# Gated cross-attention and expert block on one Trainium2 core: the attention update's bias, scale, statistics and normalisation moved between engines

## The reference

```python
hs = layernorm(x)
q, k, v = hs @ Wq.T + bq, ctx @ Wk.T + bk, ctx @ Wv.T + bv       # 16 heads of 32
probs = softmax(clip(where(mask, q @ k.T / sqrt(32), -1e4), -50, 50))
delta = clip(residual_scale, 0, 0.3) * ((probs @ v) @ Wo.T + bo)
delta = (delta - mean(delta)) / sqrt(var(delta) + 1e-5) * ln_gamma + ln_beta
x1 = x + tanh(g_xattn) * delta
h = layernorm(x1)                                                 # "h" in the kernel
out = x1 + tanh(g_ffn) * top2_of_8_experts(h)                     # router, silu(gate) * up, down
```

## Time and profile before

| | us |
|---|---|
| median of 3 runs | 996.5 (996.27 to 996.64) |
| the profiled execution | 1003.46 |
| its span, first to last instruction | 1001.7 |
| PE busy in the span | 918.4 |
| DVE busy | 471.9 |
| ACT busy | 369.5 |
| POOL busy | 256.3 |

### The profile page before, as it was taken

How to read it: one execution, slowest core, us unless ns; L and a number is a source line. 1 busy time by engine, 2 the same in 40 slices (tenths; PEclk the granted TensorE clock), 3 DMA queues, 4 the chain that set the end, 5 groups by cost and what they waited for, 6 DMA issues and landing times.

```text
span 1001.7 us, 14294 instructions
## 1 busy us (share of the span) xinstructions
PE 918.4 (92%) x4201; PEld 717.9 (72%) x4202; DVE 471.9 (47%) x796; ACT 369.5 (37%) x701; POOL 256.3 (26%) x285
## 2 busy tenths in 40 slices
PE   4979999996744999999999999999999999999994
PEld 3746667664523888888888888888888888888883
DVE  5547978777778312253263172531361254217211
ACT  3555454532132222262262262622352253226221
POOL 4033627264204121131121221312122122122121
PEclk9989998989766999999999999999999999999998
DMA  7030130203364412145153162541272136111121
GB/s 299 4 123 0 54 116 31 95 22 105 139 201 147 147 32 32 21 157 158 26 194 116 34 217 85 179 135 32 40 264 41 22 105 210 21 33 30 21 42 21
DMA packets 27904, 93.92 MB, mean 94 GB/s; under 512 B 5424, under 2 KB 5424, under 8 KB 21104
## 3 DMA queue, kind: packets, MB, share of 16 engines
q1 hardware_dynamic: 18528, 72.03, 19.4%
q0 software_dynamic: 8640, 20.62, 11.1%
q10 hardware_dynamic: 720, 1.07, 0.3%
HBM read 75.03 MB, written 18.68 MB: 94 GB/s over the span
## 4 chain that ended last, share of the span: by engine, by line
PE 80%; issue 6%; DVE 6%; POOL 2%; DMA 2%; ACT 2%; SPq 0%; DVEq 0%; POOLq 0%; ACTq 0%
PE bank L247 71%; PE bank L1284 3%; DMA xs<-in_x 2%; PE bank L1271 2%; PE bank L1157 1%; DVE rden L390 1%; DVE xr L410 1%; PE bank L1111 1%; PE bank L1123 1%; PE bank L1144 1%; DVE st L425 1%; POOL rs L747 1%; ACT hs L881 1%; PE bank L1075 1%; POOL o_lo L739 0%
## 5 line engine op out<-in xcount | busy, mean ns | idle before, releaser
L247 PE MATMUL bank<-g_hi,gt_hi 128*128 128x512 f32 x592 | 237.5, 401 | 1.6 <-DVE gt_lo L658 1.6
L247 PE MATMUL bank<-g_hi,gt_lo 128*128 128x512 f32 x592 | 234.3, 396 | 0.0
L247 PE MATMUL bank<-g_lo,gt_hi 128*128 128x512 f32 x592 | 234.3, 396 | 0.0
L688 DVE TENSOR_TENSOR hid<-silu,bank 128x256 f32<-128x256 f32 x148 | 61.4, 419 | 308.8 <-ACT silu L1037 308.8
L1037 ACT ACTIVATE silu<-bank 128x256 f32<-128x256 f32 x148 | 56.7, 383 | 255.9 <-PE bank L247 255.9
L247 PEld LDWEIGHTS bank<-g_hi,gt_hi 128*128 128x128 f32 x592 | 111.4, 188 | 27.5 <-issue 2.0
L247 PEld LDWEIGHTS bank<-g_hi,gt_lo 128*128 128x128 f32 x592 | 111.4, 188 | 27.2
L247 PEld LDWEIGHTS bank<-g_lo,gt_hi 128*128 128x128 f32 x592 | 111.6, 189 | 25.8
L843 POOL COPY g_idx<-slot_idx 128x1 int32 x37 | 6.9, 185 | 470.9 <-ACT w_nxt L1051 470.9
L247 PE MATMUL bank<-dn_hi,hd_hi 128*128 128x512 f32 x296 | 126.4, 427 | 0.0
L247 PE MATMUL bank<-dn_lo,hd_hi 128*128 128x512 f32 x296 | 116.6, 394 | 0.0
(11 more groups left out here) (218 smaller groups left out, 1308.2 us busy)
## 6 DMA issues: line engine op xcount, KB each, us to landing
raw<-in_w_exp SPq DMA_DIRECT2D x48, 1024.0 KB, 5.3
raw<-in_w_attn SPq DMA_DIRECT2D x4, 1024.0 KB, 13.6
xs<-in_x SPq DMA_DIRECT2D x4, 1024.0 KB, 6.5
xr<-in_x SPq DMA_DIRECT2D x4, 1024.0 KB, 6.2
out_rows<-xr SPq DMA_DIRECT2D x16, 256.0 KB, 2.0
h_rows<-dh SPq DMA_DIRECT2D x16, 256.0 KB, 2.1
rows<-in_b_rows ACTq DMA_DIRECT2D x1, 1024.0 KB, 13.5
c_raw<-in_ctx_t SPq DMA_DIRECT2D x1, 640.0 KB, 4.0
```

The lines of the kernel that those rows point to most:

```text
L247: mm = eng.matmul(psum, a(k), b(k), start=(first and k == 0 and j == 0), stop=(last and k == n - 1 and j == 2))
L688: dve.tensor_tensor(hid[:, p, :], silu[:, p, :], bank[p][:, 256:512], ALU.mult).then_inc(hid_done, 1)
```

## The change

1. bo enters as one more matmul of each `o_product`: the stationary tile `two_rows` is one in rows 0 and 32 and zero elsewhere, `bo_two` holds the high half of the scaled bo in row 0, its low half in row 32, and zero elsewhere.
2. The residual scale is multiplied into Wo when its halves are made.
3. The bank then holds the scaled update itself. bn_stats reads it from the bank, and (update - mean) * gamma reads it from there too; L417 and `d_ready` are gone. The bank is free after the latter (`dgam`).
4. h is normalised by ACT as x * rsh + (-mean * rsh); POOL makes the second factor, `nmh`. `normalised` is gone from DVE.
5. In the tail, ACT's order is changed: the four `normalise_h` come in, and `first_gu(1)` goes behind the last copy of h.
6. c_raw shares its memory with later tiles.

```diff
         def split_weight(w):                                    # DVE
             dve.wait_ge(w_hi_done, w + 1)
-            dve.tensor_tensor(lo, raw[:, w, :], f32(hi), ALU.subtract).then_inc(w_lo_done, 1)
+            if w == 3:
+                dve.scalar_tensor_tensor(out=lo, in0=raw[:, w, :], scalar=tg[:, 2:3], in1=f32(hi),
+                                         op0=ALU.mult, op1=ALU.subtract).then_inc(w_lo_done, 1)
+            else:
+                dve.tensor_tensor(lo, raw[:, w, :], f32(hi), ALU.subtract).then_inc(w_lo_done, 1)
...
             if u is not None:                                   # DVE, update_and_residual
-                dve.wait_ge(h_store, (n + 1) * 16 * TT)
                 dve.wait_ge(d_mm, n * TT + u + 1)
-                dve.scalar_tensor_tensor(out=dh[:, u, :], in0=bank[2 + u % 2][:, :], scalar=tg[:, 2:3],
-                                         in1=rows[:, 1, :], op0=ALU.mult, op1=ALU.add).then_inc(d_ready, 1)
+                dve.bn_stats(st6[:, u, :], bank[2 + u % 2][:, :]).then_inc(dstats, 1)
...
-            if u is not None:
-                dve.wait_ge(d_ready, n * TT + u + 1)
-                dve.bn_stats(st6[:, u, :], dh[:, u, :]).then_inc(dstats, 1)
...
-                dve.scalar_tensor_tensor(out=dh[:, u, :], in0=dh[:, u, :], scalar=mv[:, u, 0:1],
+                dve.wait_ge(h_store, (n + 1) * 16 * TT)
+                dve.scalar_tensor_tensor(out=dh[:, u, :], in0=bank[2 + u % 2][:, :], scalar=mv[:, u, 0:1],
                                          in1=rows[:, 2, :], op0=ALU.subtract, op1=ALU.mult).then_inc(dgam, 1)
-        def normalised(n, t):
-            dve.wait_ge(hrstd, n * TT + t + 1)
-            dve.tensor_scalar(dh[:, t, :], xr[:, t, :], mvh[:, t, 0:1], rsh[:, t:t + 1],
-                              ALU.subtract, ALU.mult).then_inc(h_done, 1)
...
+        dve.wait_ge(setup, 16)                                  # DVE, set-up, ahead of k_all
+        dve.tensor_scalar(bo_two[0:1, :], rows[0:1, 1, :], 1.0, None, ALU.mult).then_inc(bo_done, 1)
+        dve.tensor_scalar(bo_two[LO_ROW:LO_ROW + 1, :], rows[LO_ROW:LO_ROW + 1, 1, :], 1.0, None,
+                          ALU.mult).then_inc(bo_done, 1)
+        dve.wait_ge(bo_done, 2)
+        dve.tensor_tensor(bo_two[LO_ROW:LO_ROW + 1, :], rows[LO_ROW:LO_ROW + 1, 1, :],
+                          f32(bo_two[LO_ROW:LO_ROW + 1, :]), ALU.subtract).then_inc(bo_done, 1)
...
-        for tile in (kbd_hi, kbd_lo, vbd_hi, vbd_lo, hsel):     # POOL
+        for tile in (kbd_hi, kbd_lo, vbd_hi, vbd_lo, hsel, two_rows, bo_two):
             pool.memset(f32(tile[:]), 0.0).then_inc(setup, 1)
...
+        for i, row in enumerate((0, LO_ROW)):
+            pool.wait_ge(setup, 14 + i)
+            pool.memset(f32(two_rows[row:row + 1, :]), 1.0).then_inc(setup, 1)
...
             pool.tensor_tensor(rsh[:, t:t + 1], veh[:, t:t + 1], mhalf[:, 0:1], ALU.pow).then_inc(hrstd, 1)
+            plain(pool)
+            pool.wait_ge(hrstd, n * TT + t + 1)
+            pool.tensor_scalar(nmh[:, t:t + 1], mvh[:, t, 0:1], rsh[:, t:t + 1], -1.0,
+                               ALU.mult, ALU.mult).then_inc(hbias, 1)
...
             hi = weight_halves[w][0].rearrange("p k n -> p (k n)")   # ACT, split_weight
-            act.activation(hi, raw[:, w, :], ACT.Copy).then_inc(w_hi_done, 1)
+            if w == 3:
+                act.wait_ge(dset, 1)
+                act.activation(hi, raw[:, w, :], ACT.Copy, scale=tg[:, 2:3]).then_inc(w_hi_done, 1)
+            else:
+                act.activation(hi, raw[:, w, :], ACT.Copy).then_inc(w_hi_done, 1)
+        def normalise_h(n, t):
+            act.wait_ge(x1_done, n * TT + t + 1)
+            act.wait_ge(hbias, n * TT + t + 1)
+            act.activation(dh[:, t, :], xr[:, t, :], ACT.Identity, scale=rsh[:, t:t + 1],
+                           bias=nmh[:, t:t + 1]).then_inc(h_done, 1)
...
+                if 4 <= s < 8 and back:                         # ACT, batch: behind exp and ex_hi
+                    normalise_h(b - 1, s - 4)
                 if s == 3 and front:
                     normalise_x(b + 1)
                 if s == 4 and front:
...
         act.wait_ge(d_mm, NT)                                   # ACT, tail
+        normalise_h(NB - 1, 0)
         first_gu(0)
+        normalise_h(NB - 1, 1)
         h_copy(NB - 1, 0, tail=True)
-        first_gu(1)
+        normalise_h(NB - 1, 2)
         h_copy(NB - 1, 1, tail=True)
+        normalise_h(NB - 1, 3)
         h_copy(NB - 1, 2, tail=True)
         h_copy(NB - 1, 3, tail=True)
+        first_gu(1)
         first_gu(2)
...
             if t >= 2:                                          # PE, o_product
-                pe.wait_ge(d_ready, n * TT + t - 1)
+                pe.wait_ge(dgam, n * TT + t - 1)
...
-                              n=1, first=(k == 0), last=(k == KC - 1))
-            mm.then_inc(d_mm, 1)
+                              n=1, first=(k == 0), last=False)
+            pe.matmul(bank[2 + t % 2][:, :], two_rows[:, :], bo_two[:, :], start=False, stop=True).then_inc(d_mm, 1)
```

More of the change, by code:

```diff
@@ L39 @@
 HW = H + E
+LO_ROW = 32
 def flamingo_gated_block(nc, x, ctx_t, mask, w_attn, b_cols, b_rows, gates, gate_t, w_exp, out):
@@ L109, in flamingo_gated_block @@
         k_all = sb("k_all", [P, KC, NB * T], F32, pa)
+        crs = ExitStack()
+        c_raw = sb("c_raw", [P, KC, CT], F32, crs)
+        crs.close()
         v_all = sb("v_all", [P, NB + 1, H], F32, pa)
@@ L116, in flamingo_gated_block @@
         hsel = sb("hsel", [P, P + NH], F32R, pa)
+        two_rows = sb("two_rows", [P, P], F32R, pa)
+        bo_two = sb("bo_two", [P, H], F32R, pa)
         bsel = sb("bsel", [NH, KC, 4, HD], F32R, pa)
@@ L142, in flamingo_gated_block @@
         rsh = sb("rsh", [P, TT], F32, pa)
+        nmh = sb("nmh", [P, TT], F32, pa)
         mhalf = sb("mhalf", [P, TT], F32, pa)
@@ L222, in flamingo_gated_block @@
              "inverse_spread", "context_normalised", "o_hi_done", "o_lo_done"))
-        d_mm, d_ready, dstats, dmean, dvar, drstd, dgam, xb_done, x1_done = (sem(n) for n in
-            ("delta_product", "delta_scaled", "delta_stats", "delta_mean", "delta_var", "delta_rstd",
+        d_mm, dstats, dmean, dvar, drstd, dgam, xb_done, x1_done = (sem(n) for n in
+            ("delta_product", "delta_stats", "delta_mean", "delta_var", "delta_rstd",
              "delta_gamma", "x_with_beta", "x1_done"))
-        hstats, hmean, hvar, hrstd, h_done = (sem(n) for n in ("h_stats", "h_mean", "h_var", "h_rstd", "h_done"))
+        hstats, hmean, hvar, hrstd, hbias, h_done = (sem(n) for n in
+            ("h_stats", "h_mean", "h_var", "h_rstd", "h_bias", "h_done"))
+        bo_done = sem("delta_bias_split")
         h_tr, h_ev, lg_mm, lg_done = (sem(n) for n in ("h_transposed", "h_evacuated", "logits_product", "logits_done"))
@@ L469, in batch @@
                         ln_statistics(b + 1, range(2 * s - 2, 2 * s))
-                    if 4 <= s < 8 and back:
-                        normalised(b - 1, s - 4)
                     if s == 4 and front:
@@ L541, in _ @@
                 dve.tensor_tensor(o_lo[:, m, :], o_n[:, m % 2, :], f32(o_hi[:, m, :]), ALU.subtract).then_inc(o_l, 1)
-            for t in range(TT + 2):
-                if t <= TT:
-                    update_and_residual(NB - 1, t if t < TT else None, t - 1 if t > 0 else None)
-                if t >= 2:
-                    normalised(NB - 1, t - 2)
+            for t in range(TT + 1):
+                update_and_residual(NB - 1, t if t < TT else None, t - 1 if t > 0 else None)
             for t in range(TT):
@@ L770, in batch @@
                         add_beta(b - 1, s - 1)
-            pool.wait_ge(setup, 12)
+            pool.wait_ge(setup, 16)
             ln_inverse(0)
@@ L967, in _ @@
             x_high(0, range(2, KC))
-            act.wait_ge(setup, 12)
+            act.wait_ge(setup, 16)
             act.wait_ge(pad_store, 48)
@@ L1189, in batch @@
                         if back:
-                            pe.wait_ge(d_ready, b * TT + s - 7)
+                            pe.wait_ge(dgam, b * TT + s - 7)
                         q_product(b + 1, s - 6)
@@ L1227, in _ @@
             pe.wait_ge(kv_sb, 2 + NB + 1)
+            pe.wait_ge(bo_done, 3)
             batch(0, False, True)
@@ L1239, in _ @@
                     router(NB - 1, t - 1, tail=True)
-            pe.wait_ge(d_ready, NT)
+            pe.wait_ge(dgam, NT)
             logits_by_token(range(NT - TT))
```

5 lines of the change are left out of this document (2 added, 3 removed).

## The result

The changed kernel takes 990.53 us (median of 11 runs, 984.79 to 993.33), the kernel before 996.66 us beside it on the same chip (11 runs). The ratio of the two is 0.990, with a 95% interval of 0.988 to 0.9921: 7.9 to 12 us less, where I had forecast 4.6. The ratio is not that of the medians: these lie 6.1 us apart, the means (989.5 and 998.7) 9.2, since the executions of the two kernels spread over 8.5 and 10 us. The change repeated with other runs gave 0.9912 (0.9879 to 0.9946). One execution of the kernel before, in a later group of runs, took 1319.35 us at a mean granted clock of 0.65 and is left out of all comparisons. The profiled execution took 987.01 us, with a span of 984.8.

A forecast was written before the change was run, and what follows sets the result against it. PE was taken to bound batches 1 and 2, DVE's lateness batch 3 and the tail. Terms 0.16 + 0.6 + 0.9 - 4.3 - 2.0 = -4.6 us, from 996.5 to 991.9 us; range 987.0 to 996.5.

The forecast's parts named there:

- waits of 0.68 and 3.71 us: PE's two stops in batch 3 for ACT's copy of the transposed h; both were to go, -4.4 us.
- the one small wait: End of batch 3: a new PE wait for the copies, put in at 0.6 us.
- late release of the bank: Bank free only after dgam, some 1.1 us later; 3.7 us of slack in batch 3, so no cost.
- the 0.065 us: DVE: possible surcharge for each instruction reading a bank, total about 0.5 us worse; left out of the sum.
- matmul of the bias: PE: one more matmul per o_product, 0.23 us each at full clock, 0.43 at half; +0.92 in batches 1 and 2 each.
- Rival C: ACT becomes late, waiting for POOL's new product; second x transposes wait in batches 1 and 2; +8.2, 1000.1 us; chance 0.08.
- The tail, forecast -2.0: DVE sets the pace; three periods fall from 4.54 to 3.87 us, -0.67 each; with smaller terms -2.1, taken as -2.0.
- Batch 3, forecast -4.3: DVE's step falls below PE's: waits -4.4, half clock about -1.4, added matmuls +0.9, new wait +0.6 us.
- rival B: One half-clock stretch fewer, or an earlier clock rise in the tail: 3.0 us less, 988.9; chance 0.15.
- Batches 1 and 2: PE sets their length; added matmuls make them longer by 0.6 and 0.9 us.
- The sign of being wrong: One of three such signs: a clock column differing from before in batch 1, 2 or the tail.
- rival A: The clock takes part back: one more half-clock stretch of 6.5 us costs 3.0, giving 994.9 us; chance 0.17.

The follow-up runs named there:

- late_bank: The kernel before, with PE waiting for the gamma product (dgam) instead of the first reader before reusing a bank; 1000.51 us, ratio 1.0004.
- bias_twice: The changed kernel with the bias matmul issued twice, with 0.5 instead of 1.0 in two_rows; 989.19 us, ratio 0.9907 to the kernel before.
- first pair: The first profiled executions of the kernel before (1003.46 us) and of the changed kernel (987.01 us).
- update_in_bank: The kernel before, but L417 writes back to the bank, where bn_stats and the gamma product read it; no instruction removed; 991.97 us, ratio 0.9932.
- before: The kernel before, unedited, in its first profiled execution; 1003.46 us, span 1001.7.
- before_again: The kernel before run again without edit; 998.48 us, ratio 1.0009.
- after: The changed kernel in its first profiled execution; 987.01 us, span 984.8.
- fill_tail: The changed kernel with 26 matmuls into an unused bank ahead of the tail's spreads; 988.66 us, ratio 0.9918 to the kernel before.
- tail_order: The changed kernel with first_gu(1) back behind the first copy of h in the tail; 990.73 us, ratio 0.991 to the kernel before.
- after_again: The changed kernel run again without edit; 990.84 us, ratio 0.9912 to the kernel before.
- beta_late: The changed kernel, with POOL in the tail adding beta only after the low half of the inverted sums; 989.86 us, ratio 0.991 to the kernel before.
- second pair: The profiled executions of both kernels when run again without edit; median times 998.48 us for the kernel before, 990.84 for the changed kernel.

## Why the prediction was off

**What held.** The bound was rightly read: batch 3 and the tail gave nearly everything, the other batches and the rest next to nothing. The waits of 0.68 and 3.71 us went, and the one small wait that I had put in at 0.6 us is there with 0.65. The late release of the bank costs nothing (`late_bank`), and the trace of after has no PE wait for `dgam`. A bank as source costs no more: bn_stats 0.68 to 0.70, the product 0.742; the 0.065 us that stood beside this in the prediction is not there. The matmul of the bias costs about as put (`bias_twice`). In set-up the three one-row instructions take 0.41, 0.61 and 0.68 us and lie in an idle stretch of DVE, of which 0.52 us is left before the same xt_lo. Rival C didn't occur: in batches 1 and 2 of the trace of after PE never waits for ACT. One price was off without weight: the Identity with scale and bias takes 0.80 us when it stands alone, not the 0.73 of four in a row. POOL's product takes 0.27, within the 0.2 to 0.4.

**What failed: two terms of the sum.**

The tail, forecast -2.0, was -4.3 in the first pair of traces and 40.92 - 36.23 = -4.7 in the second. The step was "a period was 4.54 and loses L417's 0.65; the small instructions ... stay as they were: 3.87". They don't stay. The power on POOL that stands between the variance and the next residual update had been held up by the product with gamma: 0.99 to 1.07 us in the tail before, 0.55 after. From the product's start to the residual update this gave 0.44 to 0.52 us a period, 0.49 in the mean (in two of the three L441 stood in that time as well, and is gone too): 4.54 - 0.65 - 0.49 = 3.40, and 3.36 was measured. Three periods of -1.18 are -3.5, in both pairs, where -2.0 was forecast: 1.5 us that have nothing to do with the clock. The rest of the tail differs with its half clock: the first update came 0.84 and 0.32 us sooner (forecast 0.4), and the end from there to the logits changed by +0.05 and -0.80 us (forecast +0.3). I had the key in hand: the earlier trace rows shows long cases of the instructions with SBUF tensors, and I argued with it for batch 3, but only for DVE, and didn't look at POOL's row, which was in the same trace. `update_in_bank`, where only the operands changed place, shows the short power by itself.

Batch 3, forecast -4.3, was -7.4 and -6.3. The step was the clock: of the half clock in this batch, 6.8 us at 204.5 and 3.4 us behind the 3.71 us stop, I took the latter to go with the stop, for -1.4, and let the former stand. Five traces have the changed kernel's code up to the tail, three that of the kernel before (in `late_bank` but for PE's wait). Us at half clock, and the length of the batch:

| trace | half clock, batch 2 | batch 2 | half clock, batch 3 | batch 3 |
|---|---|---|---|---|
| `before`, `before_again`, `late_bank` | 6.8 in each | 55.16 to 55.19 | 10.2 in each | 53.16 to 53.18 |
| `after` | 3.4 | 54.03 | 0 | 45.76 |
| `fill_tail` | 3.4 | 54.03 | 0 | 45.81 |
| `tail_order` | 6.8 | 56.12 | 0 | 45.76 |
| `after_again` | 3.4 | 54.07 | 3.4 | 46.87 |
| `beta_late` | 3.4 | 54.04 | 6.8 | 48.74 |

The stretch behind the stop is in none of the five: that part held. The other one is absent in three and shorter in one. In `beta_late`, where all 6.8 us are there as I had assumed, batch 3 fell by 53.17 - 48.74 = 4.4 us, which is the forecast of 4.3. Without them it fell by 7.4. So the step that failed is worth 3.0 us, 0.44 us for each of the 6.8 at half clock. In my terms it is rival B's event, inside batch 3. Three traces always with 6.8 us against five with 0, 0, 0, 3.4 and 6.8 suggest that the change makes this stretch rarer; what decides on it in one execution is open. The two reciprocals that bound batch 3 in `beta_late`, and the window of batch 2 in `tail_order`, which the next paragraph uses:

```profile
189.03 3.34 DVE L402 RECIPROCAL rden<-den 16x512 f32<-16x512 f32 x1
...
237.77 3.33 DVE L402 RECIPROCAL rden<-den 16x512 f32<-16x512 f32 x1
```

```profile
137.49:193.61 56.12, 54.37 (x237) 38.27 (x237) 41.80 (x78) 30.52 (x54) 27.43 (x30) 0.94 0.18 65
```

**Batches 1 and 2** were put longer by 0.6 and 0.9 and came out 0.1 and 1.1 shorter. For batch 2 it is the clock too: in `tail_order`, with 6.8 us at half clock as before, it took 56.12 us, 0.95 longer, as forecast. The sign of being wrong that the prediction named, a clock column that differs in batch 2 or the tail, is there (0.94 and 0.97, 0.71 and 0.77). For batch 1, all at full clock, the doubled matmul says that the added four cost 0.64, so something else gave back about 0.75, where I had reckoned with "a few tenths". PE's time without work in the window fell from 1.46 to 1.06 us (53.30 - 51.84 and 53.10 - 52.04), which is 0.4 of it; the rest is open, and is no more than this batch varies by.

**The sum.** The stages of the first pair add up to -13.0 us from batch 1 to the tail (190.40 against 203.39), those of the second pair to -12.3, while the medians differ by 6.1 (996.66 and 990.53) and 8.5 (999.3 and 990.84). The rest lies in the spread of single executions: in the repeat pair, set-up and batch 0 took 81.0 us before and 84.6 after, with a half-clock stretch of 6.8 us at 68 us in the latter and none in the former; the spans (997.6 and 988.1) differ by 9.5. So a profile's stages tell what the change does where the clock is alike, and the medians tell less than these, since the clock takes part of it elsewhere. That is rival A's mechanism, in a place that I had left out because the change doesn't touch its work.

That the measured 990.53 us lies close to my 991.9 is luck. I took the difference from 996.5, the median of three runs within 0.4 us of each other, and held 2 us to be more than such runs leave open; the 72 later executions of that kernel lie between 993.2 and 1002.8 with a mean of 998.4, and the intervals here are 4 to 8 us wide. The forecast was one of a difference, and that was about half of what came.

## What to carry to other kernels

An engine can be late by another engine's operands: before costing a small instruction on the path "as it was", look at its least, median and most duration, and ask which SBUF-to-SBUF work of the neighbour runs beside it. Moving operands to a bank was worth 6.2 us here (998.2 to 991.97; by the interval 4 to 9.6) with no instruction saved, a part of it by less half clock. Where two parts of a change each bring a stage down to the next bound, only one of them pays: test each alone, and keep the simpler. When a stage becomes bound by PE again, cost what PE's clock was in it as well as its waits: name the stretches at half clock, and give the forecast with and without each. And take several executions of the kernel before as the base, with their mean clock, before calling 2 us a difference.

## What the runs showed that I had not expected

- A power of one column on GpSimd, 0.55 us alone, takes 0.99 us when a product of two SBUF tensors on VectorE runs beside it.
- Half-clock stretches of 3.4 or 6.8 us come and go in the same kernel between executions, at the same few places (in the changed kernel at about 27, 68 and 200 us; in batch 2 it had 3.4 us in four traces and 6.8 in the fifth), and with them one execution differs from the next by up to 8.5 us: the changed kernel's eleven went from 984.79 to 993.33 us. This is as much as the parts of the change are worth, and it sets what six runs can tell: their intervals are 0.6 to 0.8% wide.
- Filling PE's stop ahead of a stage brings that stage's first matmuls to full clock (0.39 against 0.62 us), but in the tail half clock came 3 us later all the same. Only ahead of the long expert loop did none follow, in one trace.
